# A fused Mamba-like layer and expert layer: the four quarters of the convolution in slots 1, 2, 3, 4 of TensorE in place of 0, 1, 3, 4

## The chip, the core and the metric

The kernel runs on one core of a Trainium2 chip. The core has four engines that compute, each with its own instruction stream: TensorE (PE in the profile, its weight loads PEld), VectorE (DVE), ScalarE (ACT) and GpSimd (POOL). SyncE (SP) issues most of the transfers. Each engine takes its instructions in the order in which they stand in its program, and they wait for each other by semaphores alone. The metric is the device time of one launch in microseconds (us), lower is better.

## The reference

The input x has 8 sequences of 1024 tokens with 256 features. Two residual layers follow each other:

```python
xz = layernorm(x) @ in_proj_w.T;  xc, z = split(xz)        # 512 channels each
u = causal_conv(xc, conv_w, 4 taps, 512 -> 512) + conv_b
dt = clip(sigmoid(u @ dt_w.T + dt_b), 1e-4, 1)
B = u @ B_w.T;  C = u @ C_w.T                               # 16 states
state = exp(clip(dt * A, -5, 5)) * state + dt * B * u + 1e-6    # per token
y = sum_n(state * C) + D * u
x = x + (y * silu(z)) @ out_w.T
# then: x = x + the two best of 8 experts (gated feed-forward, hidden 352)
#           + sigmoid gate * a shared expert, on layernorm(x)
```

## The kernel before, in words

The 8192 tokens are cut into 32 chunks of 256 tokens, four chunks to a sequence. After the chunks, a second stage runs the routed experts over tiles of 256 gathered tokens; the change does not touch it.

Every engine runs the same pattern of *bodies*. A body has 16 slots, one for each of the 16 states of the scan. In body n four chunks are in work at once: `scan` (chunk n, its recurrence), `post` (chunk n-1, what follows the scan: output projection, norm, routing, shared expert), `proj` (chunk n+1, the projections that come ahead of its scan) and `norm` (chunk n+2, the first layer norm). The order of the work on each engine is written out by hand, slot by slot; nothing is sorted by a scheduler. 33 bodies run, and 30 of them have both a `post` and a `proj`.

The work around the change, with its lines:

- **The convolution** (`proj_conv`, L552). The input projection is folded into the convolution's weights, and each product is taken in three passes of high and low parts. The 512 output channels are made in four quarters of 24 matmuls each. Quarters 0 and 1 fill the two halves of one PSUM bank (`pr_bank[1]`), quarters 2 and 3 those of the other (`pr_bank[0]`). `CONV_SLOT` says in which slot each quarter is issued.
- **u** (L847). ScalarE takes each full bank to `uT` with two activations, the *first half of u* after quarter 1 and the *second half* after quarter 3. Only then can TensorE make B and C (L570, slot 5) and dt (L563, slots 6 and 7).
- **The chain of post on TensorE.** Slot 0: the state transposes of the last two states of `post` (L600), and the down product of the shared expert of the chunk before it (`shared_down`, L685). VectorE multiplies y by the gate into `y_tok` (L1268, slot 0). Slot 1: `post_y(0)` transposes the first half of `y_tok` (L530) into a bank that it shares with the rest of post (`o_bank`). ScalarE copies that to `yT` (L875, slot 1), which frees the bank. Slot 2: `post_y(1)`, the second half, waits for the copy of the first. Slot 3: `post_out` (L616), the output projection, needs both copies. VectorE adds its result to the residual at slot 4 (L1279).
- **The scan.** For each state GpSimd makes dt·B·u (L1036), ScalarE makes the decays (L798) and copies the input of the scan with an added epsilon to PSUM (`add_eps`, L814, two halves), VectorE runs the scan (L1248) and multiplies nine of the 16 states by C (L1257), GpSimd the other seven (L1025). TensorE sums the states by transposes that accumulate (L600). The term D·u opens that sum (`skip`, L589), in slot 2.

`add_eps` of one half waits until VectorE is done with the bank, three halves back (`bank_free`), for instance until it has kept the last column of a state (L1262). Whatever stands behind it in ScalarE's program waits too.

Of the kernel before, what the change touches and what calls it, by code (L numbers as in the profile page):

```python
# [72 lines left out]
def wait(eng, sem, value):  # L73

    if not isinstance(value, int) or value > 0:
        eng.wait_ge(sem, value)
# [2 lines left out]

GU_SLOT, GATE_SLOT, GATED_SLOT = [11, 12, 14], [12, 13, 15], [13, 14, 15]  # L80
MIX_SLOT = 1
CONV_SLOT, Z_SLOT = [0, 1, 3, 4], [9, 10]


def pool_products(n):
# [11 lines left out]
def build(nc, x, wx, wconv, wz, wdt, wbc, wout, conv_b, dt_b, d_skip, a_log, wgate, wgu, wd, out):  # L97
# [6 lines left out]
    with ctx:  # L104
# [685 lines left out]
        def _(act):  # L790
# [48 lines left out]

            def project(c, slot):  # L840
                done = c.index * PROJ_USES
                if slot in (2, 5):
                    h = slot // 3
                    act.wait_ge(pr_ready, done + 2 + h)
                    for j in range(2):
                        b = 2 * h + j
                        last = af(uT[c.par][:, b, :], pr_bank[1 - h][:, j * TC:(j + 1) * TC], ACT.Identity,  # L847
                                  bias=vec[:, 0, b:b + 1])
                    last.then_inc(evac, 1)
                if slot in (7, 8):  # L850
                    h = slot - 7
                    act.wait_ge(pr_ready, done + 5 + h)
                    for j in range(2):
                        b = 2 * h + j
                        block_ = pr_bank[h][:, j * TC:(j + 1) * TC]
                        last = af(block_, block_, ACT.Tanh, scale=0.5, bias=half_b[:, b:b + 1])  # L856
                    last.then_inc(sig_ready, 1)
                if slot == 6:
                    act.wait_ge(pr_ready, done + 4)
                    wait(act, b_written, c.index * 16)  # L860
                    af(b_row[:, :], pr_bank[1][0:2 * NS, 0:TC], ACT.Copy).then_inc(evac, 1)
                    act.wait_ge(evac, (c.index + 1) * EVACS)
                    act.sem_inc(b_ready, 1)
                if slot in (10, 11):
                    k = slot - 10
                    act.wait_ge(pr_ready, done + 7 + k)

                    wait(act, y_ready, c.index * NT - NT)
                    af(zs[c.par][:, k, :], pr_bank[k][:, :], ACT.Tanh, scale=0.5).then_inc(zt_ready, 1)
# [41 lines left out]
            class Body(Phases):  # L911
                eng = act

                def start(self):
                    act.wait_ge(w_small, 16 * SMALL_LOADS)
                    af(a_exp[:, :, :], a_raw[:, :, :], ACT.Exp).then_inc(a_exp_done, 1)
                    for n in range(TAPS * KM):
                        if n == TAPS:
                            norm_apply(Chunk(0, 0))
                        if n < TAPS * KM - 1:  # L920
                            act.wait_ge(comp_mm, n + 1)
                        if n == TAPS * KM - 1:
                            act.wait_ge(pool_const, 11)
                            take_normed(Chunk(0, 0))
                            act.wait_ge(comp_mm, n + 1)
                        af(w_conv[0][:, n // KM, n % KM, :], banks[n][:, :], ACT.Copy).then_inc(comp_done, 1)
                    act.wait_ge(w_early, 16 * EARLY_LOADS)
                    af(w_z[0][:, :, :], raw_z, ACT.Copy).then_inc(comp_done, 1)
                    act.wait_ge(dve_const, 3)
                    norm_apply(Chunk(0, 1))  # L930
                    for slot in range(NS):
                        project(Chunk(0, 0), slot)
                        if slot == 8:
                            decays(Chunk(0, 0), 0)
                    add_eps(Chunk(0, 0), 0, 0)
                    add_eps(Chunk(0, 0), 0, 1)
                    decays(Chunk(0, 0), 1)
                    add_eps(Chunk(0, 0), 1, 0)
                    decays(Chunk(0, 0), 2)
                    take_normed(Chunk(0, 1))  # L940

                def __call__(self, scan, post, proj, norm):
                    def ahead(n):
                        return (None, 0) if not scan else (scan, n) if n < NS else (proj, n - NS)

                    for slot in range(NS):
                        c, n = ahead(slot + DECAY_LEAD)
                        if c:
                            decays(c, n)
                        c, n = ahead(slot + 1)  # L950
                        if c:
                            add_eps(c, n, 1)
                        if norm and slot == 4:
                            norm_apply(norm)
                        if proj:
                            project(proj, slot)
                        if post:
                            finish(post, slot)
                        if post:
                            for u in units_of(slot, GATE_SLOT):  # L960
                                gate(post, u, False)
                        if norm and slot == 14:
                            take_normed(norm)
                        if scan and slot in BY_POOL and scan.pos != 3:
                            keep_last(scan, slot)
                        c, n = ahead(slot + 2)
                        if c:
                            add_eps(c, n, 0)
# [549 lines left out]
```

## Time and profile before

| | before |
|---|---|
| median of 3 runs | 2837.96 us (2835.63 to 2843.24) |
| the profiled execution, its own time | 2837.99 us |
| its span | 2836.2 us |
| PE busy | 2515.6 us (89%) |
| POOL busy | 2237.1 us (79%) |
| DVE busy | 2229.7 us (79%) |
| ACT busy | 2030.7 us (72%) |
| stage of the chunks (134 to 2160 us) | DVE 1945.07 of 2026 us busy, POOL 1930.51, PE 1787.87, ACT 1761.27 |
| mean granted TensorE clock | 0.957 |

The span is the time from the first to the last instruction on the core; the execution's own time is 1.8 us longer. Busy shares over the whole span mix two stages. From about 75 to 2178 us the chunks run, and there VectorE and GpSimd are busy nine tenths and more of each slice; afterwards the expert tiles run, and there only TensorE and the transfers are. One body lasts 64 to 67 us. In the rows below an entry of the timeline is a run of like instructions: its start, how long it took, the engine, the line, what it writes and reads, how many, and in brackets how long the engine had been idle before it and whose work ended that. Ends of matmuls are modelled; the start of the next entry tells better when TensorE was done.

### The profile page before, as it was taken

To read this page: it belongs to the slowest core of one execution; us is meant where nothing else is said; L and a number is where in the kernel's file an instruction comes from. 1 tells how busy PE (TensorE), PEld (TensorE's weight loads), DVE (VectorE), ACT (ScalarE), POOL (GpSimd) and SP (SyncE) were. 2 spreads that over 40 slices of the span, in tenths; PEclk is the share of its full clock that TensorE was granted. 3 is DMA by queue.
4 is the path that set the end of the run, shared out by engine and by line. 5 is a ranking of instruction groups with operands and counts; after the bars stand their busy time and mean duration, and the time that the engine had idled before them with its cause. 6 is when DMAs were issued, how large, how long until landed. Compare 5 with 4: busy or idle time off the path is not lost.

```text
span 2836.2 us, 48476 instructions
## 1 busy us (share of the span) xinstructions
PE 2515.6 (89%) x15232; PEld 2200.4 (78%) x15232; DVE 2229.7 (79%) x4890; ACT 2030.7 (72%) x4675; POOL 2237.1 (79%) x1354
## 2 busy tenths in 40 slices
PE   7788888888888898988898888889887699999998
PEld 4777877777777788877787777778776488888887
DVE  2999999999999999999999999999996233333332
ACT  2888888888888888888888888888884133333332
POOL 1999999999999999999999999999994133333333
PEclk9899999999999999999999999999996899999999
DMA  4222222222222222222222322222220588888886
GB/s 177 76 82 88 79 80 87 79 80 104 88 83 82 95 79 87 87 79 80 87 80 83 105 83 83 84 94 80 87 80 15 158 199 200 202 201 202 201 200 153
DMA packets 138181, 309.62 MB, mean 109 GB/s; under 512 B 15040, under 2 KB 79680, under 8 KB 137792
## 3 DMA queue, kind: packets, MB, share of 16 engines
q1 hardware_dynamic: 110848, 270.03, 30.7%
q0 software_dynamic: 27072, 36.46, 6.5%
q8 instruction: 121, 1.98, 0.3%
q14 instruction: 140, 1.15, 0.1%
HBM read 258.42 MB, written 48.01 MB: 108 GB/s over the span
## 4 chain that ended last, share of the span: by engine, by line
PE 40%; DVE 34%; ACT 14%; issue 9%; DMA 1%; POOL 1%; DVEq 0%; SPq 0%; POOLq 0%; ACTq 0%
PE bank L667 13%; DVE bank L1248 13%; PE bank L685 9%; DVE room L1248 8%; PE bank L552 7%; DVE room L1257 6%; ACT room L798 6%; ACT bank L814 4%; PE bank L600 3%; PE bank L616 2%; PE bank L530 2%; PE bank L589 1%; PE bank L563 1%; PE bank L723 1%; ACT bank L856 1%
## 5 line engine op out<-in xcount | busy, mean ns | idle before, releaser
L1036 POOL TENSOR_TENSOR room<-dtu,b_all 128x1024 f32<-128x1024 f32 x512 | 1205.7, 2375 | 18.3 <-DVE dtu L1425 13.9
L798 ACT ACTIVATE room<-room,neg_a 128x256 f32<-128x256 f32 x2048 | 868.0, 497 | 0.8 <-DVE room L1214 0.8
L814 ACT ACTIVATE bank<-room,eps_col 128x512 f32<-128x512 f32 x1024 | 695.0, 682 | 234.7 <-DVE carry L1262 163.6
L600 PE MATMUL bank<-ident,room 128*128 128x128 f32 x4096 | 558.0, 284 | 169.3 <-POOL room L1025 85.6
L600 PEld LDWEIGHTS bank<-ident,room 128*128 128x128 f32 x4096 | 484.9, 146 | 225.6 <-POOL room L1025 95.1
L1248 DVE TENSOR_TENSOR_SCAN bank<-room,carry,bank 128x256 f32<-128x256 f32 x864 | 578.0, 734 | 20.6 <-ACT bank L814 20.1
L1025 POOL TENSOR_TENSOR room<-room,c_all 128x1024 f32<-128x1024 f32 x224 | 533.0, 2379 | 46.3 <-issue 28.8
L1162 POOL DMA_INDIRECT out<-room,ids x144 | 223.9, 1555 | 408.5 <-ACT room L996 183.7
L1327 DVE SCALAR_TENSOR_TENSOR hid<-hid,bank 128x256 f32<-128x256 f32 (+1 forms) x312 | 130.2, 417 | 420.3 <-ACT hid L909 374.5
L1248 DVE TENSOR_TENSOR_SCAN room<-room,carry,bank 128x256 f32<-128x256 f32 x672 | 448.2, 726 | 11.1 <-ACT bank L814 10.5
L552 PE MATMUL bank<-xnT,w_conv 128*128 128x256 f32 x3072 | 404.6, 288 | 7.0 <-ACT xnT L837 5.5
L667 PE MATMUL bank<-room 128*128 128x256 f32 (+1 forms) x1728 | 398.4, 380 | 2.3 <-issue 2.3
L552 PEld LDWEIGHTS bank<-xnT,w_conv 128*128 128x128 f32 x3072 | 379.7, 190 | 11.2 <-ACT xnT L837 5.8
L1257 DVE TENSOR_TENSOR room<-bank,c_all 128x512 f32<-128x512 f32 x576 | 379.7, 677 | 0.0
L667 PEld LDWEIGHTS bank<-room 128*128 128x128 f32 (+1 forms) x1728 | 308.0, 182 | 59.8 <-issue 2.6
L909 ACT ACTIVATE hid<-bank 128x256 f32<-128x256 f32 (+1 forms) x312 | 117.6, 377 | 255.5 <-PE bank L667 235.1
L667 PE MATMUL bank<-xn2T,w_gu 128*128 128x256 f32 (+1 forms) x768 | 213.1, 427 | 52.0 <-DVE base L1316 52.0
L563 PE MATMUL bank<-uT,w_dt 128*128 128x256 f32 x1024 | 231.6, 379 | 0.0
L667 PEld LDWEIGHTS bank<-xn2T,w_gu 128*128 128x128 f32 (+1 forms) x768 | 150.6, 205 | 89.4 <-DVE base L1316 59.6
L563 PEld LDWEIGHTS bank<-uT,w_dt 128*128 128x128 f32 x1024 | 189.6, 190 | 23.6 <-issue 0.4
L685 PE MATMUL bank<-room,hid 128*128 128x256 f32 (+1 forms) x864 | 198.8, 379 | 1.4 <-issue 1.4
L1248 DVE TENSOR_TENSOR_SCAN bank<-room,bank 128x256 f32<-128x256 f32 x288 | 175.7, 673 | 15.4 <-ACT bank L814 15.0
(150 smaller groups left out, 2948.3 us busy)
## 6 DMA issues: line engine op xcount, KB each, us to landing
b_all<-b_scratch SPq DMA_DIRECT2D x128, 512.0 KB, 4.0
c_all<-b_scratch SPq DMA_DIRECT2D x128, 512.0 KB, 5.2
room<-in_wgu SPq DMA_DIRECT2D x72, 704.0 KB, 5.8
room<-in_wd SPq DMA_DIRECT2D x72, 384.0 KB
room<-x_by_expert SPq DMA_DIRECT2D x72, 260.0 KB
x_in<-in_x SPq DMA_DIRECT2D x32, 256.0 KB, 6.0
x<-in_x SPq DMA_DIRECT2D x32, 256.0 KB, 2.7
out<-x SPq DMA_DIRECT2D x32, 256.0 KB, 4.3
```

What stands on the lines that cost most here:

```text
L552: last = mm(pr_bank[1 - half][:, j * TC:(j + 1) * TC], w_conv[w_part][:, t, b, col:col + P], xnT[x_part][:, b, t:t + TC], start=(n == 0 an ...
L563: last = mm(pr_bank[half][:, j * TC:(j + 1) * TC], w_dt[:, b, col:col + P], uT[c.par][:, b, :], start=(b == 0), stop=(b == KD - 1))
L600: last = mm(tr_bank[k][:, b * P:(b + 1) * P], v[n % VRING][:, b, k * P:(k + 1) * P], ident[:, :], is_transpose=True, start=False, stop=(n ...
L667: last = mm(bank[0:rows, g * TC:(g + 1) * TC], w[:, b, col:col + rows], xT[:, b, :], start=(b == 0), stop=(b == KM - 1))
L685: last = mm(dn_bank(tiled)[:, k * DM:(k + 1) * DM], hid[0:rows, hid_slot(c, m), k * P:(k + 1) * P], w[0:rows, m, :], start=(m == 0), stop= ...
L798: last = af(da[n % RING][:, b, :], dt[c.par][:, b, :], ACT.Exp, scale=neg_a[:, b, n:n + 1])
L814: af(v_slot(c, n, h)[:, :], v[n % VRING][:, 2 * h:2 * h + 2, :].rearrange("p b t -> p (b t)"), ACT.Identity, bias=eps_col[:, 0:1]).then_in ...
L1025: nc.gpsimd.tensor_tensor(out=s, in0=s, in1=row, op=ALU.mult).then_inc(pool_product, 1)
L1036: nc.gpsimd.tensor_tensor(out=v[n % VRING][:, :, :], in0=dtu[:, :, :], in1=row, op=ALU.mult) \
L1162: nc.gpsimd.indirect_dma_start(out=out[:, :], out_offset=bass.IndirectOffsetOnAxis(ap=ids[t.pos][:, k:k + 1], axis=0), in_=yt[t.par][:, k, ...
L1248: last = vec_e.tensor_tensor_scan(s, da[n % RING][:, b, :], p, init, ALU.mult, ALU.add)
L1257: vec_e.tensor_tensor(out=v[n % VRING][:, 2 * h:2 * h + 2, :], in0=v_slot(c, n, h)[:, :].rearrange("p (j t) -> p j t", j=2), in1=row, op=A ...
```

## The change

`CONV_SLOT` goes from `[0, 1, 3, 4]` to `[1, 2, 3, 4]`, so quarters 0 and 1 are issued one slot later each; quarters 2 and 3 stay. ScalarE's copy of the first half of u goes from slot 2 to slot 3; the second half stays in slot 5. Nothing is added or taken away: every engine runs the same instructions as before, in another order on TensorE and ScalarE.

```diff
-CONV_SLOT, Z_SLOT = [0, 1, 3, 4], [9, 10]
+CONV_SLOT, Z_SLOT = [1, 2, 3, 4], [9, 10]
@@ ScalarE, project
-                if slot in (2, 5):
-                    h = slot // 3
+                if slot in (3, 5):
+                    h = slot // 4
                     act.wait_ge(pr_ready, done + 2 + h)
```

On TensorE, at the start of a body in the middle of the run (slots 0 to 3): L685 is the shared expert's down product, L552 a quarter of the convolution, L530 on `y_tok` the transposes `post_y`, L589 the `skip` term, L600 on `room` the state transposes, L616 the output projection.

```order
 L685 MATMUL bank<-w_dn,hid 128x256 x6
-L552 MATMUL bank<-xnT,w_conv 128x256 x24
-L530 MATMUL bank<-ident,y_tok 128x128 x4
-L552 MATMUL bank<-xnT,w_conv 128x256 x24
-L530 MATMUL bank<-ident,y_tok 128x128 x4
-L589 MATMUL bank<-diag_d,uT 128x128 x8
-L600 MATMUL bank<-ident,room 128x128 x16
+L530 MATMUL bank<-ident,y_tok 128x128 x4
+L552 MATMUL bank<-xnT,w_conv 128x256 x24
+L530 MATMUL bank<-ident,y_tok 128x128 x4
+L589 MATMUL bank<-diag_d,uT 128x128 x8
+L600 MATMUL bank<-ident,room 128x128 x8
+L552 MATMUL bank<-xnT,w_conv 128x256 x24
+L600 MATMUL bank<-ident,room 128x128 x8
 L616 MATMUL bank<-w_out,yT 128x256 x8
```

Quarter 0 now stands behind the first `post_y` and quarter 1 behind the second `post_y`, the `skip` term and one state transpose. Up to the output projection the list holds the same work.

On ScalarE, slots 2 and 3 of such a body: L847 is the copy of the first half of u, L875 the copy of the second half of y, L814 `add_eps`, L798 the decays, L819 the kept last column.

```order
 L814 ACTIVATE bank<-room,eps_col 128x512
-L847 ACTIVATE uT<-bank,vec 128x256 x2
-L875 ACTIVATE yT<-bank 128x512
-L819 ACTIVATE carry<-room 128x4
-L814 ACTIVATE bank<-room,eps_col 128x512
-L798 ACTIVATE room<-room,neg_a 128x256 x4
-L814 ACTIVATE bank<-room,eps_col 128x512 x2
+L875 ACTIVATE yT<-bank 128x512
+L819 ACTIVATE carry<-room 128x4
+L814 ACTIVATE bank<-room,eps_col 128x512
+L798 ACTIVATE room<-room,neg_a 128x256 x4
+L814 ACTIVATE bank<-room,eps_col 128x512
+L847 ACTIVATE uT<-bank,vec 128x256 x2
+L814 ACTIVATE bank<-room,eps_col 128x512
```

The two activations of u moved behind one set of decays and two `add_eps`; the order of all the others is the same.

## Rows read from the trace of the kernel before

**Rows 1.** Waits of VectorE, 134 to 2160 us: total, times, longest
```profile
DVE bank L1248 <- ACT bank L814: 32.9, 51, 0.9
DVE room L1248 <- ACT bank L814: 15.3, 30, 0.7
DVE x L1279 <- PE bank L616: 3.4, 7, 1.0
```

**Rows 2.** The chain that ended last, slots 5 to 9 of one body: start, us
```profile
945.62 0.82 ACT uT L847 x2
...
957.73 0.04 DVE bank L1248
```

**Rows 3.** Timeline of TensorE, slots 0 to 5 of the same body
```profile
921.41 2.83 PE L685 MATMUL bank<-w_dn,hid 128*128 128x256 f32 x12 [0.39 <-issue]
923.89 3.21 PE L552 MATMUL bank<-xnT,w_conv 128*128 128x256 f32 x24
926.93 0.60 PE L530 MATMUL bank<-ident,y_tok 128*128 128x128 f32 x4
927.29 3.09 PE L552 MATMUL bank<-xnT,w_conv 128*128 128x256 f32 x24
930.22 0.60 PE L530 MATMUL bank<-ident,y_tok 128*128 128x128 f32 x4
...
934.19 3.62 PE L616 MATMUL bank<-w_out,yT 128*128 128x256 f32 x16
...
941.29 3.12 PE L552 MATMUL bank<-xnT,w_conv 128*128 128x256 f32 x24
```

**Rows 4.** Timeline of VectorE, the same body, slots 0 and 4
```profile
923.80 1.26 DVE L1268 SCALAR_TENSOR_TENSOR y_tok<-bank,zs 128x512 f32<-128x512 f32 x2
...
939.71 0.67 DVE L1279 TENSOR_TENSOR x<-bank,x 128x512 f32<-128x512 f32 x1
```

**Rows 5.** Timeline of ScalarE, the same body, slots 1 and 5
```profile
928.38 0.69 ACT L814 ACTIVATE bank<-room,eps_col 128x512 f32<-128x512 f32 x1 [2.04 <-DVE carry L1262]
929.01 0.58 ACT L875 ACTIVATE yT<-bank 128x512 f32<-128x512 f32 x1
...
944.99 0.69 ACT L814 ACTIVATE bank<-room,eps_col 128x512 f32<-128x512 f32 x1 [1.44 <-DVE carry L1262]
```

**Rows 6.** Timeline of TensorE in the first body that has a post
```profile
140.75 0.63 PE L530 MATMUL bank<-ident,y_tok 128*128 128x128 f32 x4 [0.73 <-ACT yT L875]
```

**Rows 7.** Timelines of TensorE and ScalarE in the next body
```profile
995.79 0.60 ACT L875 ACTIVATE yT<-bank 128x512 f32<-128x512 f32 x1 [0.18 <-PE bank L530]
...
998.45 0.60 PE L530 MATMUL bank<-ident,y_tok 128*128 128x128 f32 x4
...
1012.65 0.84 ACT L847 ACTIVATE uT<-bank,vec 128x256 f32<-128x256 f32 x2 [0.42 <-PE bank L552]
```

**Rows 8.** The same two engines in a body that starts a sequence
```profile
1127.34 0.58 ACT L875 ACTIVATE yT<-bank 128x512 f32<-128x512 f32 x1
...
1129.82 0.60 PE L530 MATMUL bank<-ident,y_tok 128*128 128x128 f32 x4
...
1144.04 0.84 ACT L847 ACTIVATE uT<-bank,vec 128x256 f32<-128x256 f32 x2 [0.86 <-PE bank L552]
```

**Rows 9.** Waits of all engines, 134 to 2160 us: total, times, longest
```profile
PE bank L570 <- ACT uT L847: 12.7, 11, 1.2
...
ACT uT L847 <- PE bank L552: 9.1, 16, 0.9
```

**Rows 10.** Timeline of VectorE in the body without a post
```profile
98.92 1.27 DVE L1248 TENSOR_TENSOR_SCAN bank<-room,bank 128x256 f32<-128x256 f32 x2 [0.87 <-ACT bank L814]
```

**Rows 11.** Timeline of TensorE after pauses of several lengths
```profile
74.82 5.49 PE L552 MATMUL bank<-xnT,w_conv 128*128 128x256 f32 x24 [5.52 <-ACT xnT L837]
...
969.41 1.99 PE L667 MATMUL bank<-xn2T,w_gu 128*128 128x256 f32 x8 [2.21 <-DVE base L1316]
...
987.96 4.51 PE L685 MATMUL bank<-w_dn,hid 128*128 128x256 f32 x12 [0.40 <-issue]
```

## The prediction, made before the changed kernel ran

> **What bounds the kernel now.** The table of stages in the profile is read first: between 134 and 2160 us VectorE is busy 1945 of 2026 us, so it all but sets the pace there, and each microsecond that it waits is paid. Then the waits of VectorE [rows 1]: it waits almost only for ScalarE's `add_eps` (32.9 + 15.3 us in 81 waits), and seven times, 3.4 us together, for TensorE's output projection at slot 4. GpSimd is almost as busy but no row has VectorE waiting for it. Then the chain that ended last [rows 2]: in slots 5 to 9 it leaves VectorE and runs through ScalarE, from just ahead of the second half of u (945.62) until VectorE takes over again at 957.73. So in these slots a later start of the second half of u is paid in full by the scan. Two dates of a body can hurt: the second half of u on ScalarE, which waits for quarter 3, and L1279 on VectorE, which waits for the output projection. Both hang on how late TensorE is when it has come through slots 0 to 3.
>
> **TensorE's order in slots 0 to 3.** The work from the shared expert's down product to the output projection is the same before and after, so only new pauses shift what follows.
>
> Before, quarter 0 covers the time in which VectorE makes `y_tok`, and quarters 0 and 1 together cover the time until ScalarE has made the first `yT`. Take the body at 923.80. The down product is followed at 923.89 by quarter 0 [rows 3]; `y_tok` is ready at 923.80 + 1.26 = 925.06 [rows 4]. With `post_y(0)` next in line TensorE pauses from 923.89 to about 925.1, 1.2 us. It then takes 0.36 us (926.93 to 927.29), quarter 0 another 3.04 (923.89 to 926.93), so it stands before `post_y(1)` at 928.5. That one needs the first `yT`, and ScalarE's copy ends at 929.01 + 0.58 = 929.59 [rows 5]. The copy doesn't come earlier when the transpose does: it stands behind an `add_eps` that waited 2.04 us for VectorE and started at 928.38 [rows 5]. So `post_y(1)` starts at 929.64, a second pause of 1.1 us. Counted from there, quarter 1 (2.93, 927.29 to 930.22) is still to do, while before it was done when `post_y(1)` started at 930.22. TensorE is late by 929.64 + 2.93 - 930.22 = 2.35 us from there on.
>
> That this wait is real is seen in the first body with a post: there `post_y(0)` and one quarter preceded `post_y(1)` without another quarter in hand, and TensorE waited 0.73 us for `yT` [rows 6].
>
> Late by 2.35, the output projection ends at 934.19 + 3.62 + 2.35 = 940.16, where VectorE comes for it at 939.71 [rows 4]: 0.45 us. Quarter 3 ended at 941.29 + 3.12 = 944.41 and ScalarE took the second half of u at 945.62 [rows 3, 2]: 1.21 us of slack, so it now starts 2.35 - 1.21 = 1.14 us later. The two don't add up: VectorE's first 0.45 us makes ScalarE's next wait (1.44 us ahead of the `add_eps` at 944.99 [rows 5]) end later by as much, which is still before quarter 3 is done. This body pays 1.14 us.
>
> In other bodies TensorE is late already. In the next one `post_y(1)` started at 998.45; the copy for it ended at 995.79 + 0.60 = 996.39, after a wait of 0.18 for the transpose, which now comes early, so 996.2 [rows 7]. `post_y(1)` starts at 996.26, plus quarter 1 gives 999.19, late by 0.74 us. Here ScalarE waited 0.42 us for quarter 3 before the second half of u [rows 7], so there is no slack, and 0.74 is paid. In the body that starts a sequence: 1127.34 + 0.58 + 0.05 + 2.93 - 1129.82 = 1.08 us, again with a wait for quarter 3 (0.86), so 1.08 is paid [rows 8]. Which kind a body is, the waits count: TensorE waited for u in 11 bodies, ScalarE for quarter 3 in 16 [rows 9]; the 3 bodies left I put with the second kind. 11 x 1.14 = 12.5 us; 19 x 0.9 (the middle of 0.74 and 1.08) = 17.1 us. The first body with a post comes on top: its `post_y(1)` stays where it is, so all of quarter 1 (2.93) is the delay instead of 2.35, 0.6 us more.
>
> **ScalarE's order.** The first half of u (0.82 us, as long as the second in [rows 2]) leaves slot 2 and enters slot 3. In slot 2 no one gains: VectorE has no wait there. In slot 3 it needs quarter 1, which now ends at 929.64 + 0.44 + 1.8 (`skip`) + 0.9 (one state transpose) + 2.93, about 935.7, while ScalarE comes to it behind a set of decays and an `add_eps` more than before. The 0.82 us, and a short wait for quarter 1 if there is one, are swallowed in the 1.44 us of waiting ahead of 944.99 [rows 5]. If that cover were gone they would be paid, and in the body without a post they are: that body lacks the slots' work of a post, its slack isn't read, and VectorE waits 0.87 us for ScalarE there already [rows 10]. I put 0.8 us, once; its bounds are 0 and 0.82.
>
> GpSimd, the weight loads and all transfers keep their order. B and C, written a microsecond later, are wanted only in slot 11. The state transposes of the first two states end at about 932.7 and 936.6 instead of 934.2; GpSimd wants the ring places that they free eight states on, in slots 3 and 4, and no engine waits for GpSimd's product in the waits of VectorE [rows 1].
>
> **Sum.** 12.5 + 17.1 + 0.6 + 0.8 = 31.0 us. The profiled execution took 2837.99 us (span 2836.2 and 1.8 around it), which is the median of the runs shown within 0.03 us. 2838.0 + 31.0 = 2869.0, forecast 2869 us. Bounds: if the pause before the first `post_y` alone were paid (late by 1.24 in the 11, swallowed by 1.21 of slack), nothing would be left; if every microsecond of TensorE's lateness were paid, 11 x 2.35 + 17.1 + 1.4 = 44 us, 2882. I take the value between, since slack and waits are read from rows of the same body.
>
> **Rivals.**
>
> *No wait for `yT`.* If ScalarE's copy came as soon as the transpose was there, `post_y(1)` would find the bank free, only the pause of 1.2 us would be left, and only in the 11 bodies whose slack is 1.21: 2838 to 2840 us, no change. For it: TensorE is often behind anyway. Against it: the copy's place behind the `add_eps` [rows 5] and the wait in [rows 6]. It decides as soon as the copy ends before 928.5 in the body shown. Chance 8%.
>
> *The clock.* The pauses are new, and the granted clock falls after some pauses. After 5.52 us idle a quarter took 5.49 us at 1.2 GHz instead of 3.2 at 2.4; after the pauses around 986 the 12 products of the down product took 4.51 instead of 2.83; but after 2.21 us idle at 969.41 the products kept the full clock [rows 11, 3]. If quarter 0 ran at 1.2 GHz in every body, it would cost 2.3 us, of which the second pause (1.1) takes a part; with the slower transposes 1.4 us are left, 30 times, 42 us: 2911 us. The longest single new pause is 1.2 us, of which I see no case with a fall. Chance 8%.
>
> The Trainium skill speaks for this rival: "Perfetto Trace Analysis", section "Matmul Optimizations", says that the matmul engine scales its power with utilization and that matmuls should come back to back in batches. By that rule breaking the run of quarters with two pauses costs more than the pauses. The trace bears it out for the longer pauses and not for the one of 2.21 us.
>
> *Faster.* The scan's waits in slots 7 to 9 are ScalarE's backlog. If that backlog came from slot 2, taking 0.82 us out of it there would bring each `add_eps` of slots 7 to 9 forward by as much: 30 x 0.82 = 25 us less, 2813 us. It decides if ScalarE runs from slot 2 to slot 9 without a wait. It doesn't: it waits 1.44 us in slot 5 [rows 5], and the same 0.82 comes back in slot 3. It would also need quarter 3 to be in time. Chance 4%.
>
> **How the numbers follow.** The forecast's case has 80%, no wait 8%, the clock 8%, faster 4%. About 0.3% (8.5 us) is what a measurement of this kernel can tell from no change, so: slower 88%, same 8%, faster 4%. Range: the forecast's case by itself reaches from half of the sum (other slack in bodies that I haven't read) to the upper bound, 2853 to 2884. Taking in a part of the neighbours: 2850 to 2892.
>
> **What would show it.** In the changed kernel TensorE waits for `y_tok` (L1268) ahead of L530 in about a third of the bodies, near 1.2 us each, and for `yT` (L875) ahead of L530 in nearly all, 0.4 to 1.1 us each; before, [rows 6] was an exception. VectorE waits for L616 at L1279 in most bodies, 0.4 to 1 us. ScalarE waits for quarter 3 (L552) ahead of the second half of u in all 30, not 16, and TensorE's own wait ahead of L570 for the same reason stays. VectorE's waits for `add_eps` grow from 48 us to some 60 and those for L616 from 3.4 to some 20. A body lasts 1 us longer. The mean clock stays at 0.96. I'm wrong if the second half of u starts where it did, or if the quarters show the half clock often.

## The result

| | before | changed |
|---|---|---|
| median | 2837.95 us (2835.63 to 2843.24, 4 runs) | 2870.32 us (2869.54 to 2872.45, 4 runs) |
| ratio to before | | 1.0107, 95% interval 1.0091 to 1.0122 |
| profiled execution | 2837.99 us, span 2836.2 | 2872.45 us, span 2870.7 |
| mean granted TensorE clock | 0.957 | 0.956 |

The changed kernel is 32.4 us slower; 31.0 were forecast (2869 us, range 2850 to 2892). Rows of before are named by their group.

**TensorE**, timeline of the same body as in [rows 3], whose gate product now starts at 937.13:

```profile
934.74 2.83 PE L685 MATMUL bank<-w_dn,hid 128*128 128x256 f32 x12 [0.39 <-issue]
938.44 0.66 PE L530 MATMUL bank<-ident,y_tok 128*128 128x128 f32 x4 [0.87 <-DVE y_tok L1268]
938.85 3.09 PE L552 MATMUL bank<-xnT,w_conv 128*128 128x256 f32 x24
943.05 0.63 PE L530 MATMUL bank<-ident,y_tok 128*128 128x128 f32 x4 [1.11 <-ACT yT L875]
943.52 1.95 PE L589 MATMUL bank<-diag_d,uT 128*128 128x128 f32 x16
...
946.10 3.09 PE L552 MATMUL bank<-xnT,w_conv 128*128 128x256 f32 x24
...
949.90 3.62 PE L616 MATMUL bank<-w_out,yT 128*128 128x256 f32 x16
```

Both pauses are there, in brackets: 0.87 us before the first transpose and 1.11 before the second. The second transpose of y starts 5.92 us after the gate product (943.05 - 937.13); 5.84 were worked out (929.64 - 923.80). The output projection starts at 12.77 us, where it had been at 10.39 [rows 3]: late by 2.38, forecast 2.35.

**ScalarE and VectorE**, timelines of the same body (answers to [rows 4, 5]):

```profile
941.70 0.69 ACT L814 ACTIVATE bank<-room,eps_col 128x512 f32<-128x512 f32 x1 [2.04 <-DVE carry L1262]
942.33 0.58 ACT L875 ACTIVATE yT<-bank 128x512 f32<-128x512 f32 x1
...
949.99 0.69 ACT L814 ACTIVATE bank<-room,eps_col 128x512 f32<-128x512 f32 x1 [1.47 <-DVE carry L1262]
950.61 0.82 ACT L847 ACTIVATE uT<-bank,vec 128x256 f32<-128x256 f32 x2
...
958.87 0.69 ACT L814 ACTIVATE bank<-room,eps_col 128x512 f32<-128x512 f32 x1 [1.31 <-DVE carry L1262]
960.13 0.84 ACT L847 ACTIVATE uT<-bank,vec 128x256 f32<-128x256 f32 x2 [0.57 <-PE bank L552]
```

```profile
937.13 1.26 DVE L1268 SCALAR_TENSOR_TENSOR y_tok<-bank,zs 128x512 f32<-128x512 f32 x2
...
953.55 0.69 DVE L1279 TENSOR_TENSOR x<-bank,x 128x512 f32<-128x512 f32 x1 [0.43 <-PE bank L616]
```

The first transpose of y is now done early, and ScalarE's copy of it (942.33) still stands behind the same `add_eps` with the same wait of 2.04 us. The first half of u (950.61) waits for nothing. The second half starts 23.00 us after the gate product; it was 21.82, and 22.96 was worked out. VectorE waits 0.43 us for the output projection, forecast 0.45.

**The waits of the whole stage** (134 to 2193 us; total, times, longest; answers to [rows 1, 9]):

```profile
DVE bank L1248 <- ACT bank L814: 41.3, 65, 0.9
PE bank L530 <- ACT yT L875: 27.4, 27, 3.8
DVE x L1279 <- PE bank L616: 23.9, 31, 1.6
ACT uT L847 <- PE bank L552: 18.4, 30, 0.8
DVE room L1248 <- ACT bank L814: 15.9, 30, 0.7
PE bank L530 <- DVE y_tok L1268: 11.0, 12, 1.4
POOL room L1036 <- PE bank L600: 7.4, 11, 1.2
```

VectorE, which sets the pace, waits 41.3 + 15.9 + 23.9 = 81.1 us where it waited 51.6 [rows 1]: 29.5 us more. The last row is all but new: GpSimd waits for a ring place, which it did once before, for 0.5 us. The two traces differ by more than the medians, 34.5 us of span (2870.7 - 2836.2). Of the rest, 3.7 us are busy time of VectorE (1948.76 us from 134 to 2193, against 1945.07 from 134 to 2160); what made it isn't shown. The gate product of the first body with a post comes at 135.6 instead of 134.8 us, but over all traces of this case it starts between 132.9 and 137.1, so the 0.8 us that were forecast for the body without a post are neither shown nor refuted.

From one gate product to the next, the 30 bodies with a `post` and a `proj` last 32.9 us longer in all. The ten that were like the one shown take 1.19 to 1.49 us more each, 12.6 together; the first body with a post 2.05; the other 19 between 0.22 and 1.52, 18.2 together.

**The chain that ended last**, the same body:

```profile
953.52 2.85 PE bank L552 x24
956.37 0.88 PE bank L600 x8
957.25 2.86 PE bank L552 x24
960.11 0.03 issue
960.13 0.02 ACT uT L847
```

It ran through VectorE up to slot 5 before and came to ScalarE from there [rows 2]; now it comes to the second half of u from TensorE, whose work from the second transpose of y on is all on it.

### The profile page after: what moved, and what is told of

It is laid out like the page before. It is cut to its first block, busy times and chain, and to the rows that moved or that the text cites. A ratio compares the mean times of both kernels' runs of the same rounds, so it can differ in the third digit from the quotient of the medians.

```text
span 2870.7 us, 48476 instructions
## 1 busy us (share of the span) xinstructions
PE 2522.8 (88%) x15232; PEld 2197.4 (77%) x15232; DVE 2233.6 (78%) x4890; ACT 2030.4 (71%) x4675; POOL 2237.5 (78%) x1354
## 4 chain that ended last, share of the span: by engine, by line
PE 42%; DVE 32%; ACT 15%; issue 9%; DMA 1%; POOL 1%; SPq 0%; DVEq 0%; ACTq 0%; POOLq 0%
PE bank L667 13%; DVE bank L1248 12%; PE bank L552 9%; DVE room L1248 7%; PE bank L685 7%; DVE room L1257 6%; ACT room L798 6%; ACT bank L814 5%; PE bank L616 4%; PE bank L600 3%; PE bank L530 2%; PE bank L589 2%; PE bank L563 1%; DVE y_tok L1268 1%; PE bank L723 1%
## 5 line engine op out<-in xcount | busy, mean ns | idle before, releaser
L814 ACT ACTIVATE bank<-room,eps_col 128x512 f32<-128x512 f32 x1024 | 696.9, 683 | 261.9 <-DVE carry L1262 185.3
L798 ACT ACTIVATE room<-room,neg_a 128x256 f32<-128x256 f32 x2048 | 868.5, 498 | 0.8 <-DVE room L1214 0.8
L600 PE MATMUL bank<-ident,room 128*128 128x128 f32 x4096 | 561.9, 284 | 174.2 <-POOL room L1025 89.3
L600 PEld LDWEIGHTS bank<-ident,room 128*128 128x128 f32 x4096 | 486.0, 146 | 230.2 <-POOL room L1025 98.5
L552 PE MATMUL bank<-xnT,w_conv 128*128 128x256 f32 x3072 | 401.3, 286 | 7.0 <-ACT xnT L837 5.5
L552 PEld LDWEIGHTS bank<-xnT,w_conv 128*128 128x128 f32 x3072 | 377.4, 190 | 9.6 <-ACT xnT L837 5.8
L685 PE MATMUL bank<-room,hid 128*128 128x256 f32 (+1 forms) x864 | 198.8, 379 | 1.4 <-issue 1.4
```

The lines of the kernel that those rows point to most:

```text
L552: last = mm(pr_bank[1 - half][:, j * TC:(j + 1) * TC], w_conv[w_part][:, t, b, col:col + P], xnT[x_part][:, b, t:t + TC], start=(n == 0 an ...
L600: last = mm(tr_bank[k][:, b * P:(b + 1) * P], v[n % VRING][:, b, k * P:(k + 1) * P], ident[:, :], is_transpose=True, start=False, stop=(n ...
L685: last = mm(dn_bank(tiled)[:, k * DM:(k + 1) * DM], hid[0:rows, hid_slot(c, m), k * P:(k + 1) * P], w[0:rows, m, :], start=(m == 0), stop= ...
L798: last = af(da[n % RING][:, b, :], dt[c.par][:, b, :], ACT.Exp, scale=neg_a[:, b, n:n + 1])
L814: af(v_slot(c, n, h)[:, :], v[n % VRING][:, 2 * h:2 * h + 2, :].rearrange("p b t -> p (b t)"), ACT.Identity, bias=eps_col[:, 0:1]).then_in ...
```

## The experiments

The theory: TensorE is late because the second transpose of y waits for ScalarE's copy with nothing left to do, and this lateness is paid at the second half of u and at L1279. The rivals: ScalarE's new order, the clock, and the place of the quarters in itself. Ratios are to before, run on the same chip in the same sitting, with their 95% intervals. Where an experiment adds lines, line numbers of the profile are 2 higher (4 in e7 and e11).

**e1_scalar_only**: ScalarE's half of the change alone.

```diff
-                if slot in (2, 5):
-                    h = slot // 3
+                if slot in (3, 5):
+                    h = slot // 4
```

> ScalarE's half of the change alone: TensorE's quarters stay in slots 0, 1, 3, 4, the first half of u is copied in slot 3. My theory (TensorE's two new pauses are the cost): the 0.82 us are swallowed in the wait of slot 5 in all bodies but the one without a post; 2838 to 2840 us. Rival (the load on ScalarE in slots 3 to 9 is the cost): 30 bodies times up to 0.8 us, 2855 to 2862 us.

Measured 2840.78 us, ratio 1.0004 (0.9995 to 1.0014). ScalarE's order by itself costs nothing that can be measured; the 15 us and more of the rival are out.

**e2_tensor_only**: TensorE's half alone.

```diff
-CONV_SLOT, Z_SLOT = [0, 1, 3, 4], [9, 10]
+CONV_SLOT, Z_SLOT = [1, 2, 3, 4], [9, 10]
```

> TensorE's half alone: quarters in slots 1, 2, 3, 4, ScalarE still takes the first half of u in slot 2. ScalarE comes to it at 8.5 us after the gate product and quarter 1 is ready only at 12.0, so ScalarE stands for 3.5 us with the decays and copies of state 4 behind it. My theory: VectorE waits about 2.7 us in slot 4 and the bodies are 2.5 to 3 us longer than before, 2910 to 2925 us; so ScalarE's half of the change is what keeps the cost down. Rival (the order on ScalarE costs nothing either way): as the changed kernel, 2870 us.

Measured 2894.15 us, ratio 1.0199 (1.0182 to 1.0217). Both were wrong in size, mine by some 16 us and the rival by 24: each body lost 1.9 us, not 2.5 to 3. ScalarE and VectorE in slots 2 to 4 of the same body (timelines):

```profile
958.04 0.84 ACT L847 ACTIVATE uT<-bank,vec 128x256 f32<-128x256 f32 x2 [3.56 <-PE bank L552]
```

```profile
960.17 1.39 DVE L1248 TENSOR_TENSOR_SCAN room<-room,carry,bank 128x256 f32<-128x256 f32 x2 [0.84 <-ACT bank L814]
...
962.26 1.38 DVE L1248 TENSOR_TENSOR_SCAN room<-room,carry,bank 128x256 f32<-128x256 f32 x2 [0.71 <-ACT bank L814]
```

ScalarE stands for 3.56 us as expected, but VectorE waits 0.84 + 0.71 = 1.55 us: ScalarE had been some 2 us ahead of it, further than I counted. So moving the copy of u with the quarters saved some 24 us of what TensorE's half alone costs (2894.2 to 2870.3).

**e3_both_in_slot1**: quarter 1 between the two transposes of y as well.

```diff
-CONV_SLOT, Z_SLOT = [0, 1, 3, 4], [9, 10]
+CONV_SLOT, Z_SLOT = [1, 1, 3, 4], [9, 10]
...
-                if slot in CONV_SLOT:
-                    n = CONV_SLOT.index(slot)
-                    proj_conv(c, n // 2, n % 2)
+                for n in range(4):
+                    if CONV_SLOT[n] == slot:
+                        proj_conv(c, n // 2, n % 2)
```

> Quarters 0 and 1 both in slot 1, between the two transposes of y; the first half of u stays in slot 2. The first new pause (for y_tok) stays, the second (for the copy of y) goes, since quarter 1 covers it. My theory: TensorE is late by 1.2 us only in the bodies where it has 1.2 us of slack; 2838 to 2842 us. Rival (the first pause or a lower clock after it costs): 11 to 30 bodies times 1.2 us, 2851 to 2874 us.

Measured 2839.91 us, ratio 1.0006 (0.9995 to 1.0017). TensorE still pauses for `y_tok`, as its waits show (the same view as above):

```profile
PE bank L530 <- DVE y_tok L1268: 12.7, 14, 1.4
```

So the first pause, by itself, is free: 12.7 us of it cost nothing that can be measured. The second is the one that counts.

**e4_yT_first**: the changed kernel with ScalarE's first copy of y ahead of the waiting `add_eps`.

```diff
+                        if post and slot == 1:
+                            finish(post, slot)
                         c, n = ahead(slot + 1)
                         if c:
                             add_eps(c, n, 1)
...
-                        if post:
+                        if post and slot != 1:
                             finish(post, slot)
```

> The changed kernel, with ScalarE's first copy of y taken ahead of the add_eps of slot 1 that waits 2 us for VectorE. The copy then ends near 3.1 us after the gate product begins instead of 5.8, and the second transpose of y doesn't wait. My theory: most of the loss comes back, 2838 to 2842 us, with quarters still in slots 1, 2, 3, 4. Rival (quarters behind the skip term and the state transpose are late by themselves, or the clock): it stays at 2860 to 2870 us.

Measured 2838.93 us, ratio 0.9998 (0.9988 to 1.0008), with the quarters still in slots 1, 2, 3, 4. All of the loss is back. Of the waits for `yT` ahead of a transpose one of 1.1 us is left, and those for `y_tok` stay:

```profile
PE bank L530 <- DVE y_tok L1270: 14.7, 16, 1.6
```

**e9_skip_first**: the changed kernel, with the pause filled and ScalarE left alone.

```diff
-                        if post and slot in (1, 2):
-                            post_y(post, slot - 1)
                         if slot == 2 and scan:
                             skip(scan)
+                        if post and slot in (1, 2):
+                            post_y(post, slot - 1)
```

> The changed kernel, with the skip term (16 matmuls, 1.8 us on TensorE, which depends on neither copy) moved ahead of the second transpose of y. It fills the second pause (1.1 us); ScalarE's program is untouched. My theory: TensorE's lateness falls to that of the first pause, 1.2 us in the bodies that have 1.2 us of slack, so 2838 to 2843 us. Rival (it is the copy's date, not TensorE's standing idle, or the clock): 2860 to 2870 us.

Measured 2839.82 us, ratio 1.0002 (0.9992 to 1.0011). The copy of y is as late as in the changed kernel (5.21 us after the gate product in the body shown, 5.20 there); TensorE only has 1.8 us of other work in hand. With e4 this closes it from both ends: either the date of the copy or TensorE's want of work can be taken away, and all 32 us are gone.

**e5_0234**: quarter 0 back in slot 0.

```diff
-CONV_SLOT, Z_SLOT = [0, 1, 3, 4], [9, 10]
+CONV_SLOT, Z_SLOT = [0, 2, 3, 4], [9, 10]
...
-                if slot in (2, 5):
-                    h = slot // 3
+                if slot in (3, 5):
+                    h = slot // 4
```

> Quarters in slots 0, 2, 3, 4, first half of u in slot 3. Quarter 0 covers the time of y_tok again, so the first pause goes, but nothing but the transpose is left in slot 1, and TensorE then waits for the copy of y until 5.85 us as in the changed kernel. My theory (the copy of y alone sets when TensorE goes on): the same as the changed kernel, 2868 to 2872 us, with one pause of up to 2.4 us. Rival (each pause is paid by itself): a third or more of the loss comes back, 2850 to 2860 us.

Measured 2888.15 us, ratio 1.0166 (1.0149 to 1.0183): 18 us slower than the changed kernel, which neither side expected. Two bodies of its timeline with the same pause:

```profile
949.81 0.63 PE L530 MATMUL bank<-ident,y_tok 128*128 128x128 f32 x4 [2.19 <-ACT yT L875]
950.27 3.31 PE L589 MATMUL bank<-diag_d,uT 128*128 128x128 f32 x16
...
1019.24 0.63 PE L530 MATMUL bank<-ident,y_tok 128*128 128x128 f32 x4 [2.19 <-ACT yT L875]
1019.70 1.95 PE L589 MATMUL bank<-diag_d,uT 128*128 128x128 f32 x16
```

The two pauses of the changed kernel are here one of 2.19 us. Behind it the skip term takes 3.31 us in one body and 1.95 in the other: the granted clock is 0.55 of 2.4 GHz there (950.27 to 953.40), close to the level of 1.2 GHz, and 1.00 in the other (1019.70 to 1021.50). Of the 30 bodies with all four quarters ten are like the first. The last body, without quarters, has it too, but so it has before and after the change. In the body shown VectorE's L1279 waits 2.10 us and comes 1.7 us later after the gate product than in the next one. The ten bodies last 1.56 to 1.68 us longer than in the changed kernel, 16.0 us together, and the other 20 together 2.2. So the clock rival was alive, not at the pauses of this change but one step beside it: in e5 the longest of VectorE's waits reads

```profile
DVE x L1279 <- PE bank L616: 42.5, 31, 2.9
```

18.6 us more than after the change.

**e10_0234_skip_first**: e5 with the skip term moved as in e9.

> e5_0234 (2888 us) with the skip term ahead of the second transpose of y, so its pause of 2.4 us shrinks to about 0.6. e5 lost 18 us more than the changed kernel; in four of its bodies the trace shows the output projection 1.5 us later than in the others. If that is the granted clock, which falls after the pause of 2.4 us, both losses go: 2838 to 2848 us. Rival (something else in the order 0, 2, 3, 4 costs the 18 us): 2855 us or more.

Measured 2839.92 us, ratio 0.9999 (0.9989 to 1.0008). The wait for `yT` fell from 54.4 us in 31 waits to 7.7 in 14, and with it both losses went. The 18 us come from the pause. That it is the clock is read from the rows of e5, where the same pause of 2.19 us stands in both bodies; this run doesn't separate the clock from the length of the pause.

**e6_quarter_begun**: before, with two of quarter 0's passes issued where TensorE waits for VectorE.

```diff
                         if slot == 0 and post:
                             state_transpose(post, NS - 2)
+                            if proj:
+                                proj_conv(proj, 0, 0, PASSES[:2])
                             state_transpose(post, NS - 1)
...
-                            project(proj, slot)
+                            project(proj, slot, bool(post))
```

(`project` then gives `proj_conv` only `PASSES[2:]` for quarter 0.)

> The kernel before, with the first two of quarter 0's three passes (16 matmuls) issued between the last two state transposes, where TensorE waits 0.7 to 3.6 us for VectorE in every body. My theory (TensorE's lateness at quarter 3 is paid wherever ScalarE waits for it, 16 bodies, 9 us, and the output projection's 3 us): TensorE is up to 2 us earlier in the late bodies, 2826 to 2832 us, and ScalarE's waits for quarter 3 are gone. Rival (slots 5 to 9 are set by ScalarE's load whatever TensorE does): 2837 to 2839 us.

Measured 2824.01 us, ratio 0.9942 (0.9926 to 0.9959), a little better than expected. ScalarE's wait for quarter 3 is gone (no row of L552 in its waits), and VectorE's waits shrink to 24.4 + 15.1 for `add_eps` and 0.5 for the output projection. A part that I had not counted: the work stands where TensorE paused for up to 3.6 us, and the shared expert's down product after it now takes longer than the 2.84 us of full clock in 2 of 31 bodies instead of 21 of 31, 89.4 us in all instead of 111.6. No run tells how much of the 16 us is the clock's.

**e7_begun_u_first**: e6, and the second half of u at the start of slot 5.

```diff
+                        if proj and slot == 5:
+                            project(proj, slot)
                         c, n = ahead(slot + 1)
                         if c:
                             add_eps(c, n, 1)
...
-                        if proj:
+                        if proj and slot != 5:
                             project(proj, slot)
```

> As e6_quarter_begun, and ScalarE takes the second half of u at the start of slot 5, ahead of the add_eps that waits 1.4 us for VectorE. If quarter 3 is in time in all bodies (about 20.0 us after the gate product begins, ScalarE comes at 20.6), the chain through ScalarE starts 0.45 us earlier in each of 30 bodies: 13 us below e6, 2812 to 2820 us. Rival (quarter 3 still late in some bodies, so the copy of u blocks the add_eps): 2835 us or more.

Measured 2810.44 us, ratio 0.9894 (0.9878 to 0.9911): 14 us below e6 (13 forecast), and 1.6 us under my range. But the condition of the forecast failed: quarter 3 is not in time, ScalarE waits for it in all 30 bodies.

```profile
ACT uT L849 <- PE bank L552: 23.3, 30, 2.3
```

So the time came out and the mechanism didn't: the move gains although ScalarE stands for 0.8 us a body.

**e8_u_first**: the second half of u at the start of slot 5, TensorE as before.

> The kernel before, with only ScalarE's second half of u at the start of slot 5, TensorE as before. In the 11 bodies where quarter 3 is early it gains 0.45 us each, in the 19 others ScalarE stands before an add_eps until quarter 3 is done and loses about 0.7: my theory 2840 to 2850 us. Rival (the place in slot 5 doesn't matter): 2838 us.

Measured 2847.46 us, ratio 1.0025 (1.0015 to 1.0034), inside my range. ScalarE's wait for quarter 3 (134 to 2160 us):

```profile
ACT uT L847 <- PE bank L552: 64.0, 30, 4.2
```

The same move on ScalarE wins 14 us where it waits 0.8 us a body for quarter 3 (e7), and loses 7 where it waits 2.1.

**e11_begun_u_skip_first**: e7 with the skip term moved as in e9.

> e7_begun_u_first (2810 us) with the skip term ahead of the second transpose of y. TensorE waits there 1.1 us for the copy in nearly every body, and ScalarE then waits 0.5 to 1 us for quarter 3. Filling the pause makes quarter 3 early enough; but ScalarE's next add_eps waits for VectorE at nearly the same time, so only bodies that start a sequence gain: 2803 to 2810 us. Rival (ScalarE's wait for quarter 3 is the last one and all of it comes back): 2790 to 2798 us.

Measured 2808.30 us, ratio 0.9887 (0.9871 to 0.9904), 32 us below before. From e7 it isn't told apart: the intervals of the two ratios overlap. Its waits of TensorE and ScalarE:

```profile
PE bank L616 <- ACT yT L877: 29.8, 31, 1.3
...
ACT uT L849 <- PE bank L552: 22.3, 30, 2.4
```

The pause was not removed but moved: TensorE now waits ahead of the output projection, for the second copy of y. So quarter 3 is no earlier, and ScalarE waits for it as in e7 (22.3 us against 23.3). My range was met by luck: filling the pause was to make quarter 3 early enough, and it didn't.

## Why the prediction was right

- **The two pauses.** Forecast 1.2 and 1.1 us in the body shown, 0.87 and 1.11 in the profile's brackets; the transposes start where they were expected within 0.1 us. The first shows in 12 bodies (about a third forecast), the second in 27 (nearly all forecast). That the copy of y doesn't come earlier held, and it is what the loss hangs on: e4 and e9 each take back all of it, e3 shows the first pause to be free.
- **Where it is paid.** The second half of u at 23.00 us after the gate product against 22.96, ScalarE's wait for quarter 3 in 30 bodies against 16, VectorE's wait at L1279 in 31, 23.9 us (some 20 forecast), its waits for `add_eps` 57.2 us (some 60 forecast). A little more of the loss than forecast is paid at L1279.
- **The two kinds of body.** The slack of 1.21 us in 11 bodies and none in 19 was the step that kept the sum from 44 us. No run varied the slack by itself, but the lengths of the bodies show it: the 11 in which TensorE waited for u before (the ten and the first one above) lost 14.7 us, forecast 12.5 + 0.6; the other 19 lost 18.2, forecast 17.1.
- **The two bodies behind the 0.9 us.** These two missed, and here the sum had some luck. The next body lost 1.44 us (forecast 0.74), the one that starts a sequence 1.52 (forecast 1.08). In neither does the second pause occur. TensorE comes to the second transpose late by itself, since the down product ran below full clock for longer than before: 5.46 us instead of 4.51, and 4.79 instead of 3.29 (granted clock over it 0.50 instead of 0.59, and 0.56 instead of 0.82). The mean of the 19 (0.96) was close all the same; 15 of the other 17 have the pause. The next body:

```profile
1002.48 5.46 PE L685 MATMUL bank<-w_dn,hid 128*128 128x256 f32 x12 [0.37 <-issue]
...
1011.54 0.60 PE L530 MATMUL bank<-ident,y_tok 128*128 128x128 f32 x4
```

- **ScalarE's order.** Forecast: swallowed in 1.44 us of waiting. Shown by e1, and by the row at 950.61, where the copy waits for nothing, while the wait ahead of 958.87 is still 1.31 us (VectorE came 0.4 us later too).
- **The rival of the clock.** Wrong for the quarters of this change: the mean clock went from 0.957 to 0.956, and of the 120 quarters in the stage of the chunks none took over 3.26 us. Beside the quarters the clock has a small part: the 31 down products take 114.5 us together instead of 111.6, and two of them are those above. How much of the 2.9 us is paid isn't shown. The Trainium skill's advice ("Perfetto Trace Analysis", "Matmul Optimizations") to run matmuls back to back in batches agrees with e5, where half clock behind a pause of 2.1 us and more made ten bodies 1.6 us longer, and with the down products of e6, which filled a pause.
- **Small misses.** I said that TensorE's wait ahead of L570 would stay; it is gone from the list of TensorE's own waits (12.7 us before), since ScalarE now takes u as soon as quarter 3 ends and a state transpose covers it. And GpSimd does wait for ring places, 7.4 us in 11 waits where the forecast saw none: the later state transposes free them late. No wait of ScalarE or VectorE for GpSimd grew, so there is no sign that it was paid.

## What to carry to other kernels

Before moving work on an in-order engine, ask what the instruction that it uncovers waits for, and on which other engine that work stands behind a wait: the copy here was ready to be made 3 us earlier, but stood behind an instruction that waited for a third engine. Independent work belongs between a producer and its consumer; the skip term, which depends on neither copy (16 matmuls in the profile), was worth 32 us in the right place and nothing in the wrong one. Lateness is only paid beyond the slack that the waits of the next consumer show, so the sum is made for each kind of iteration, not for one.

## What the runs showed of the hardware

- In e5 17 of the 30 bodies have a pause of 2.12 us or more ahead of the second transpose of y. Behind it the skip term ran at half clock in ten of them (3.07 to 3.45 us) and at full clock in seven (1.95 us); two bodies with the same pause of 2.19 us differ in it. Behind the 13 shorter pauses (0.78 to 1.21 us) it always took 1.95 us.
- In the changed kernel the pauses of up to 1.4 us ahead of the two transposes were followed by no slow skip term in the 30 bodies, and no quarter took over 3.26 us (before, none over 3.22). In the last body, behind a pause of 3.84 us, the skip term took 3.23 us.
- With 16 matmuls in a pause of 0.7 to 3.6 us (e6), the profile shows a mean clock of 0.966 instead of 0.957, on top of the work that it hid.
